# A decoder layer on one core: operands taken as they land, splits and clamps moved to GpSimd, a new order of units

## The reference

```python
def _L0_attn_ref(x, Wq, bq, Wk, bk, Wv, bv, Wo, bo):
    q = split_heads(x @ Wq + bq); k = split_heads(x @ Wk + bk); v = split_heads(x @ Wv + bv)
    att = jnp.einsum('bhqd,bhkd->bhqk', q, k) * scale            # hd = 16
    att = jax.nn.softmax(jnp.where(tril, att, -jnp.inf), axis=-1)
    return merge(jnp.einsum('bhqk,bhkd->bhqd', att, v)) @ Wo + bo
def _weight_quant(w):
    scale = 1.0 / jnp.clip(jnp.mean(jnp.abs(w)), 1e-05)
    wq = jnp.clip(jnp.round(w * scale), -1.0, 1.0) / scale        # ternary
def _L0_ffn_ref(x, w_gate, w_up, w_down):
    gate = jax.nn.silu(_bitlinear(x, w_gate)); up = _bitlinear(x, w_up)
    return _bitlinear(gate * up, w_down)
x = _layernorm(x + attn(x)); x = _layernorm(x + xattn(x, ctx)); x = _layernorm(x + ffn(x))
```

## Time and profile before

| | us |
|---|---|
| median of 3 runs | 849.23 (847.72 to 849.62) |
| the profiled execution, its own time | 847.58 |
| its span, first to last instruction | 845.5 |
| TensorE busy, weight loads apart | 797.8 (94%) |
| VectorE, ScalarE, GpSimd busy | 687.9, 574.6, 342.9 |
| mean granted TensorE clock | 0.996 |

### The profile page before, as it was taken

How to read it: one execution, slowest core, us unless ns; L and a number is a source line. 1 busy time by engine, 2 the same in 40 slices (tenths; PEclk the granted TensorE clock), 3 DMA queues, 4 the chain that set the end, 5 groups by cost and what they waited for, 6 DMA issues and landing times.

```text
span 845.5 us, 20914 instructions
## 1 busy us (share of the span) xinstructions
PE 797.8 (94%) x7816; PEld 395.7 (47%) x7816; DVE 687.9 (81%) x1261; ACT 574.6 (68%) x751; POOL 342.9 (41%) x582
## 2 busy tenths in 40 slices
PE   8889999999999989999999999999999999999997
PEld 6534345344564434534454344543545443445645
DVE  4899998948998699887999689974899848836698
ACT  1277856467965588655885679866597579864595
POOL 3832454344333055431544245442425403552344
PEclk9999999999999999999999999999999999999999
DMA  7422102100211011100131020101110001010001
GB/s 233 94 83 58 46 20 72 42 21 3 49 47 58 1 41 38 26 26 10 40 87 26 11 79 2 39 11 29 39 52 2 8 1 52 2 51 1 2 2 52
DMA packets 37189, 32.90 MB, mean 39 GB/s; under 512 B 9828, under 2 KB 33252, under 8 KB 37092
## 3 DMA queue, kind: packets, MB, share of 16 engines
q1 hardware_dynamic: 33844, 28.93, 12.2%
q0 software_dynamic: 1536, 1.58, 0.8%
q10 hardware_dynamic: 1712, 1.05, 0.5%
HBM read 14.55 MB, written 4.19 MB: 22 GB/s over the span
## 4 chain that ended last, share of the span: by engine, by line
PE 64%; DVE 20%; ACT 6%; issue 5%; POOL 2%; ACTq 1%; DMA 0%; SPq 0%; POOLq 0%; DVEq 0%
PE ps L1031 12%; DVE shift L1376 11%; PE ps L826 8%; PE ps L1016 7%; PE ps L994 6%; PE ps L839 5%; PE ps L965 3%; PE ps L790 3%; PE ps L977 3%; PE ps L892 3%; PE ps L922 2%; PE ps L917 2%; PE ps L815 2%; PE ps L934 2%; ACT probs L1137 2%
## 5 line engine op out<-in xcount | busy, mean ns | idle before, releaser
L1376 DVE TENSOR_REDUCE shift<-ps 128x2 f32<-128x1024 f32 (+2 forms) x320 | 343.9, 1111 | 39.6 <-PE ps L994 19.4
L1137 ACT ACTIVATE probs<-ps 128x1024 f32<-128x1024 f32 (+3 forms) x384 | 294.2, 811 | 103.9 <-PE ps L1016 101.4
L1031 PE MATMUL ps<-probs,v_aug 128*32 128x512 f32 (+3 forms) x1536 | 157.5, 499 | 0.1
L705 POOL TENSOR_SCALAR_AFFINE_SELECT probs<-probs 128x512 f32<-128x512 f32 x128 | 80.7, 640 | 163.8 <-ACT probs L1137 163.0
L994 PE MATMUL ps<-k_stack,q_stack 48*128 48x512 f16 (+3 forms) x768 | 114.6, 330 | 13.2 <-DVE shift L1376 4.8
L1016 PE MATMUL ps<-q_stack,k_stack 49*128 49x512 f16 (+3 forms) x768 | 116.0, 328 | 10.4 <-DVE shift L1376 4.9
L1016 PEld LDWEIGHTS ps<-q_stack,k_stack 49*128 49x128 f16 x768 | 37.6, 93 | 112.9 <-ACT probs L1137 37.9
L994 PEld LDWEIGHTS ps<-k_stack,q_stack 48*128 48x128 f16 x768 | 40.3, 93 | 97.2 <-DVE shift L1376 34.5
L1000 PE MATMUL ps<-causal,pick_h 64*128 64x64 bf16 x1024 | 53.3, 190 | 0.0
L1078 ACT ACTIVATE full<-ps,bias_scaled,kq_scale 128x512 f32<-128x512 f32 x32 | 25.0, 780 | 41.5 <-PE ps L839 32.3
L1000 PEld LDWEIGHTS ps<-causal,pick_h 64*128 64x128 bf16 x1024 | 46.4, 96 | 14.4 <-issue 0.5
(11 more groups left out here) (205 smaller groups left out, 1361.0 us busy)
## 6 DMA issues: line engine op xcount, KB each, us to landing
q_stack<-part_sb SPq DMA_DIRECT2D x168, 32.0 KB, 2.0
k_stack<-part_sb SPq DMA_DIRECT2D x144, 32.0 KB, 2.0
xT<-in_x_cols SPq DMA_DIRECT2D x8, 512.0 KB, 4.5
xt<-in_x SPq DMA_DIRECT2D x8, 512.0 KB, 4.1
out_x<-xt SPq DMA_DIRECT2D x7, 512.0 KB, 3.5
q_stack<-shiftT SPq DMA_DIRECT2D x128, 1.0 KB
k_stack<-part_sb POOLq DMA_DIRECT2D x48, 32.0 KB, 2.0
region<-in_w_gate SPq DMA_DIRECT2D x4, 256.0 KB, 4.2
```

Source lines behind the costliest of these rows:

```text
L705: pool.affine_select(out=blk, in_=blk, compare_op=ALU.is_ge, fill=0.0, base=0, pattern=[[0, HG], [1, P]], channel_multiplier=-1).then_inc( ...
L1031: mm = pe.matmul(ps[DV * i:DV * (i + 1), SUM_BANK, off:BANK], v_aug[:, kb, at:at + DV], probs_of(b, n)[:, i, :], start=first, stop=last)
L1137: act.activation(probs_of(b, n)[:, 2 * p:2 * p + 2, :], pair(u)[:, :, 0:BANK - off], ACT.Exp, scale=exp_scale).then_inc(probs_ready, 1)
L1376: dve.tensor_reduce(to[:, :, pairs[0]:pairs[-1] + 1, qb % TH], pair(u)[:, :, 0:len(pairs) * w].rearrange("p j (h w) -> p j h w", w=w), AX. ...
```

## The change

Five things are changed.

1. `tops` of batch 0 no longer waits for `consts_ready`: VectorE takes the maximum of w_k, of the first half of x, of w_q, of the second half, each behind the wait for that operand alone, then the bias sums. The wait for `consts_ready` is now in `take_bound` (and on TensorE in `bound`).
2. TensorE runs 36 transposes instead of 70, then the first of the two matmuls (d = 0) of the four pieces 0 to 3, into banks 0 to 3, and then `bound`; the second matmuls follow where the pieces stood. ScalarE runs a one-element activation as soon as `round_c` is there, in front of which its table load now falls.
3. Pieces 4 to 7 of batch 0 are split by GpSimd, as in the later batches (cast and subtraction), no longer by ScalarE and VectorE.
4. The clamp of the ternary weights is on GpSimd, in front of its cast.
5. `ORDER` is new throughout, with 58 stirs instead of 70.

```diff
-STIRS = 70
+STIRS = 58
+WARM_UP = 36
 ORDER = (
-    "ffrr6r0sr6sz0ffr0r6wr0ssffgr6m01m23ggm45r6gm23m01m45r6m01r2m45m01m23r6m01m45a23a01aw6a23z4w4a01m23aa56om01m4"
+    "rr6r0sr1sr2r3r6ssgggfr1fffr6wm01fffgm23m45r6m23m01m45m23r6z4ffm45m23m01r6xm23z4fa01fm45a23w6aa01w4a23sm01am5"
...
-    "vvv23pu0ptu6uv23v1v6vutz0z0z6z6vz6z6z6z6z6z6z6t"
+    "45pv2v3vz6z6z6z6tz6uvtt"
 )
...
-                if (b, n) == (1, 0):
-                    pool.wait_ge(low_ready, NP)
+                if (b, n) == (0, SLOTS):
+                    pool.wait_ge(low_ready, SLOTS)
...
                 if u.kind == "tern":
                     n = u.idx
+                    pool.wait_ge(tern_rounded, n + 1)
+                    pool.tensor_scalar(raw[n], raw[n], ROUND - 1.0, ROUND + 1.0, ALU.max, ALU.min).then_inc(tern_ready, 1)
                     pool.wait_ge(tern_ready, n + 1)
...
-                if u.kind == "split" and u.b > 0:
+                if u.kind == "split" and (u.b > 0 or u.idx >= SLOTS):
                     split(u.b, u.idx)
...
+            begun = [n for n in range(SLOTS) if not find["kq", 0, n].before]
+            def project(u, ds):
+                t, e, h = pieces[u.idx]
+                if u.b == 0:
+                    pe.wait_ge(kq_loaded[1 - t], 16)
+                pe.wait_ge(x_loaded[h], 16 * (u.b + 1))
+                for d in ds:
+                    mm = pe.matmul(ps[:, u.bank, :], (wk, wq)[t][:, d, e * P:(e + 1) * P],
+                                   xT[:, h, d, :], start=(d == 0), stop=(d == CC - 1))
+                return mm
...
                 if kind == "kq":
+                    mm = project(u, [d for d in range(CC) if b > 0 or d > 0 or u.idx not in begun])
                 elif kind == "bound":
                     if b == 0:
-                        stir(u, 70)
+                        stir(u, WARM_UP)
+                        for n in begun:
+                            project(find["kq", 0, n], [0])
+                        pe.wait_ge(consts_ready, 1)
                     pe.wait_ge(tops_ready, b + 1)
...
+            act.wait_ge(pool_ready, 5)
+            act.activation(first_out[:], round_c[:], ACT.Identity, bias=round_c[:, 0:1])
...
-                if u.kind == "split" and u.b == 0:
+                if u.kind == "split" and u.b == 0 and u.idx < SLOTS:
...
                 for h in range(QC):
+                    if b == 0:
+                        dve.wait_ge(kq_loaded[1 - h], 16)
+                        link(dve.tensor_reduce(w_top[:, :, h], (wk, wq)[h][:], AX.X, ALU.max, apply_absolute_value=True))
                     dve.wait_ge(x_loaded[h], 16 * (b + 1))
                     link(dve.tensor_reduce(x_top[:, h, :], xT[:, h, :, :], AX.X, ALU.max, apply_absolute_value=True))
                 link(dve.tensor_tensor(x_top[:, QC, :], x_top[:, 0, :], x_top[:, 1, :], ALU.max))
+                for t, bias in enumerate((bk_c, bq_c)) if b == 0 else ():
+                    dve.wait_ge(bias_loaded[1 - t], 16)
+                    link(dve.tensor_reduce(b_sum[:, t:t + 1], bias[:], AX.X, ALU.add, apply_absolute_value=True))
...
             dve.memset(v_aug[:], 1.0)
-            dve.wait_ge(consts_ready, 1)
-            for t, bias in enumerate((bk_c, bq_c)):
-                dve.wait_ge(bias_loaded[1 - t], 16)
-                link(dve.tensor_reduce(b_sum[:, t:t + 1], bias[:], AX.X, ALU.add, apply_absolute_value=True))
-            for t, w in enumerate((wk, wq)):
-                dve.wait_ge(kq_loaded[1 - t], 16)
-                link(dve.tensor_reduce(w_top[:, :, t], w[:], AX.X, ALU.max, apply_absolute_value=True))
...
-                if u.kind == "split" and u.b == 0:
+                if u.kind == "split" and u.b == 0 and u.idx < SLOTS:
                     low(u.idx)
...
-                if u.kind == "tern":
-                    n = u.idx
-                    dve.wait_ge(tern_rounded, n + 1)
-                    dve.tensor_scalar(raw[n], raw[n], ROUND - 1.0, ROUND + 1.0, ALU.max, ALU.min).then_inc(tern_ready, 1)
```

86 lines of the change are left out of this document (40 added, 46 removed).

## The result

The changed kernel takes **858.05 us** (median of 6 runs, 855.64 to 860.84), the kernel before 849.42 us in the same session (6 runs, 847.70 to 852.86). The ratio is 1.0098, with a 95% interval of 1.0068 to 1.0127: the change makes the kernel 8.6 us slower, where 841.2 us were forecast and 834.5 to 847.5 us given as the range. The profiled execution took 857.69 us, its span is 856.0 us.

The account below looks back on a forecast made before the run. TensorE was taken as the limit from 127 to 750 us, VectorE closer from 40 to 127, latencies in the first 29. Span 845.5 - 4.5 - 3.0 - 0.5 = 837.5 us; median 849.23 - 8.0 = 841.2 us, range 834.5 to 847.5.

Parts of the forecast that it names:

- the price of the clamp: Ternary clamp on GpSimd: taken as 1.90 us from the cast's row, with 1.9 to 4.4 us kept as range.
- Rival (a): GpSimd sets the pace in batch 0: 4.4 us clamps hold masks back 2.4 us, no VectorE relief; 846.6 us, 14%.
- Hidden, at no cost: Batch 1's first split, behind w_down's clamp on GpSimd: delayed 5.9 us (8.4 at the far price), covered by 8.4 us.
- Term A: Start, up to the first maxima: earlier bound and table load bring them 4.5 us sooner; -4.5 us, bounds -1.3 and -6.5.
- Term B: Batch 0, mainly 40 to 127 us: VectorE loses low parts and clamps to GpSimd; -3.0 us, bounds 0 and -6.8.
- Term C: The end, 800 to 838.4 us: four stirs instead of ten, most returning as waiting; -0.5 us, bounds 0 and -3.1.
- Term D: Order of units elsewhere: neighbours change places, nothing seen to gain or lose; 0 us, bounds +3 and -3.
- Rival (c): Batches 1 to 3: SP's moves stand closer to the maxima needing them and begin late; +12 us, 853.2 us, 6%.
- The clock: TensorE's granted clock at start and end: falls folded into the bounds, 1.7 us each, six needed to end slower.

Follow-up runs that it names:

- e9: Changed kernel with GpSimd's three clamps replaced by differing test operations; maximum and minimum together took 7.08 us, add and multiply 1.89 us; no kernel time given.
- e13: Changed kernel with each of GpSimd's three clamps replaced by adding 0 and multiplying by 1, the clamp itself left out; 843.88 us.
- e6: Kernel before, with its order, clamps and splits, and only the new start, two half pieces ahead of the bound instead of four; 846.61 us.
- e7: Kernel before, with its order and clamps on VectorE, plus the start of e6 and pieces 4 to 7 of batch 0 split by GpSimd; 843.39 us.
- e4: Changed kernel with pieces 4 to 7 of batch 0 split by ScalarE and VectorE again, the clamp staying on GpSimd; 864.44 us.
- e1: Changed kernel with the three ternary clamps back on VectorE, at the same units of the new order; 846.83 us.
- e8: e1 with each clamp placed one reduction later in VectorE's order; 845.04 us.
- e2: Kernel before with only the three ternary clamps moved to GpSimd, ahead of its casts; 864.12 us.
- e3: Changed kernel with each of GpSimd's three clamps of 2048 columns cut into eight of 256, back to back; 867.08 us.
- e10: e8 with 20 more transposes on TensorE just ahead of the first maxima; 845.94 us.
- e11: e7 with 60 instead of 36 transposes ahead of the bound; 844.92 us.

## Why the prediction was wrong, point by point

**The failing step: the price of the clamp.** "I take 1.90 us, since form and length agree and only the output is wider, and keep 1.9 to 4.4 us." The cast and the clamp do agree in form and length, and the output's width costs nothing (e9). What differs is the pair of operations, add and multiply against maximum and minimum, and no row had a maximum over many columns on GpSimd. The range between two rows of other operations was no bound. 7.1 us instead of 1.90 us, three times, made 14.2 us (858.05 against 843.88 in e13). The sentence from the Trainium skill, "GPSIMD Engine Reference", section 8, with its 2.4 us by a factor of two to VectorE, pointed to the right side but is off by three times too: the row of VectorE is 1.22 us, so this operation is 5.8 times slower on GpSimd. I had noted that it spoke against the move, and gave that no weight.

**Rival (a) was the mechanism**, at the wrong size: with clamps of 4.4 us it gave 846.6 us. The masks came not 2.4 us later but 4.6 us (110.28 us for 105.7 us before), from a kernel that had been 3.3 us ahead. A second path was missing from the prediction altogether: the clamp as it ran on GpSimd held VectorE's steps on the shifts. "Hidden, at no cost" for w_down's clamp fails by that path and not by the one that was weighed. Rounding, clamp and cast are 2.1 + 7.1 + 1.9 = 11.1 us against 8.4 us of cover, yet from 136 to 190 us TensorE has no wait over 0.1 us for a move; its wait of 5.13 us was for two held steps of VectorE.

**Term A, the start**, was right in every step that it named: bound 11.34 us (11.3), first piece 13.35 us (13.4); the first maxima came at 22.79 us, 1.6 us before the forecast, so the quicker landing that I had kept for the range did come (2.50 us for 4.00 us). What failed is the step from there to the end: "whatever shortens it moves all later work with it, as long as that work waits for nothing else". It did wait for other things. Of 6.1 us, 3.3 us were left at 93 us. The kernel with the start alone gained 2.9 us (e6), not 4.5 us; its start is the smaller one of two half pieces, with a lead of 4.0 us at the first maxima.

**Term B, relief of VectorE**: the four splits alone gave 3.2 us (e7) and 6.4 us (e4), against -3.0 us for splits and clamps together. The splits were worth at least the whole term, the clamps had the other sign.

**Term C, the end**: from reduction 368 to the end it is 87.1 us after and 87.6 us before, 0.5 us less as forecast. **Term D, the order**: from reduction 80 to 368 the changed kernel gained 2.1 us, within its bounds of 3 us. That is not the whole of it. e1 and e8 have start, splits and clamps where e7 has them (but for two half pieces and the clamps' exact place) and differ in the order: they took 3.4 and 1.7 us more than e7, with intervals that overlap. One cause is in the traces: the hold of 3.63 us near 500 us stands in nine of the ten traces of the new order that keep that step's form, and in none of the five of the old order (0.58 us at most). The changed kernel is the tenth (0.51 us); that it missed this hold was luck. Rival (c), SP's moves too close to their maxima, did not happen.

**The clock**: "one fall costs 1.7 us, and it would take six to end slower" took falls as a matter by themselves. They followed the waits: in the windows from 88 to 150 us the clock is 0.77 to 0.86, and there the work behind TensorE's waits ran slower too. The three long waits add to 12.2 us, the stretch lost 16.5 us.

With 1.89 us for the clamp the time would have lain in the range (843.88 us measured, 841.2 us forecast), though partly by luck: the start gave less than its term and the splits more. The chances would still have been too sure, since one unseen price carried the sign, and 86% for faster rested on it.

## What to carry to other kernels

An operation that no row shows is bounded by rows of the same arithmetic on the same engine, not by rows of the same shape; if there are none, say that the price is open, ask at which price the sign turns, and measure it first. For work that moves to GpSimd, list what is queued behind it there and who waits for that, and list VectorE's small steps beside it as well. A lead won at the start pays only as far as the next shared resource lets it through: in e13, 3.0 us of 6.0 us at the end.

## What the runs showed of the hardware

- On GpSimd a maximum, a minimum or both with constants over 128 x 2048 elements take 5.4, 5.4 and 7.1 us, add and multiply 1.89 us (e9); the pair took as long in bf16 as in f32. VectorE's row for the same clamp is 1.22 us.
- A long operation on GpSimd holds some of VectorE's: `tensor_scalar` and `tensor_tensor` on 2 to 16 columns took up to 4.48 us (e4, at 129.81 us) for 0.17 us. Reductions were not held: in the changed kernel, e2, e4 and e9 none beside a clamp took over 1.5 times its usual time. The Trainium skill, "SBUF — State Buffer", section "Who interferes with whom", says that VectorE shares a port pair with GpSimd and that an operation with two SBUF inputs, or in a mode that uses both port pairs, contends with GpSimd, that in such a mode the later of the two waits for the whole of the other, and that a reduction never contends; by that, the traces agree on who is held. They differ on how long. At 499.92 us in e8 the hold went on over several operations in a row, 3.63 us. Two-input steps were let go before the clamp's end, at 132.88 us with a clamp that ran from 128.37 to 135.44 us, in e9 at 113.01 us with one from 108.50 to 115.58 us, and once in e4, 4.51 us after its start all three times; e9's next two-input step, at 113.05 us, took 0.16 us beside the same clamp:

```profile
109.04 3.97 DVE L1375 TENSOR_TENSOR x_top<-x_top 128x2 f32<-128x2 f32 x1
```

- Cut into pieces of 256 columns back to back, the same clamp left four of the five small steps that fell beside it at 0.16 to 0.18 us and the fifth at 0.34 us (e3), at 9.0 us for 7.1 us in sum. Why seven operations in a row held at 500 us and these did not was not tried.
- Filling a wait of 2.1 us with transposes took away the fall of the granted clock at 24 us, but the next one, 3.4 us from 41.7 us in e8, became one of 10.2 us from 39.1 us, behind a wait of 3.19 us (e10). In e11, too, the fall at 11.9 us went and one came at 25.8 us.
